# A graph network on one core: two pairs of VectorE steps change places in the attention stages

## The reference

```
# second layer: masked attention, 12 heads of 32
q, k, v = h @ Wq + bq, h @ Wk + bk, h @ Wv + bv
scores = q k^T / sqrt(32) + beta * adj ; where(adj > 0, scores, -9e15)
x = x + softmax(scores) v
# fourth layer: attention with an additive bias and an output projection
a = (h Wq^T)(h Wk^T)^T * 384**-0.5 + bias
a = where(all of a row == 0, -inf, a) ; a = nan_to_num(softmax(a))
x = x + (a v) Wo^T + bo
```

## Time and profile before

| | us |
|---|---|
| median of 3 runs | 2972.63 (2971.61 to 2974.18) |
| the profiled execution | 2975.63 |
| its span | 2973.9 |
| TensorE busy (matmul) | 2791.2 (94%) |
| VectorE busy | 1962.7 (66%) |
| ScalarE busy | 1033.1 (35%) |
| GpSimd busy | 950.6 (32%) |

### The profile page before, as it was taken

One profiled execution on the slowest core, in us unless ns is written; L12 is line 12 of the kernel. 1 busy time (PEld: TensorE's weight loads), 2 busy tenths in 40 slices (PEclk: granted clock), 3 DMA queues, 4 the chain that ended last, 5 costly groups with the idle time before them and its releaser, 6 DMA issues.

```text
span 2973.9 us, 64342 instructions
## 1 busy us (share of the span) xinstructions
PE 2791.2 (94%) x26048; PEld 2336.2 (79%) x26048; DVE 1962.7 (66%) x4550; ACT 1033.1 (35%) x1985; POOL 950.6 (32%) x874
## 2 busy tenths in 40 slices
PE   6999999999989999999999998999998799999997
PEld 5888878888868888887878877888887678777786
DVE  4444445555566777778676666676777777777775
ACT  2443333333334444443232322222222344343442
POOL 1222213444443333332010110343343444443443
PEclk9999999999999999999999999999999999999999
DMA  3222333333321121131211223223232011111011
GB/s 93 74 72 72 95 101 107 102 97 100 121 70 48 48 71 48 48 95 55 70 60 57 70 76 103 74 73 97 91 100 90 31 47 48 47 48 44 32 33 35
DMA packets 197320, 211.45 MB, mean 71 GB/s; under 512 B 72736, under 2 KB 197024, under 8 KB 197024
## 3 DMA queue, kind: packets, MB, share of 16 engines
q1 hardware_dynamic: 197024, 207.33, 22.7%
HBM read 131.80 MB, written 75.50 MB: 70 GB/s over the span
## 4 chain that ended last, share of the span: by engine, by line
PE 71%; DVE 17%; issue 8%; ACT 2%; POOL 2%; DMA 0%; DVEq 0%; SPq 0%; POOLq 0%; ACTq 0%
PE psum L672 27%; PE psum L675 26%; DVE v_x L1502 4%; PE psum L723 3%; PE psum L990 3%; DVE room L1650 2%; PE psum L660 2%; PE psum L840 2%; PE psum L885 2%; PE psum L829 2%; DVE room L1640 2%; DVE room L1533 2%; PE psum L739 1%; PE psum L861 1%; DVE fast L1373 1%
## 5 line engine op out<-in xcount | busy, mean ns | idle before, releaser
L675 PE MATMUL psum<-fast 128*128 128x384 f32 x5760 | 1128.4, 345 | 91.2 <-DVE room L1640 37.9
L675 PEld LDWEIGHTS psum<-fast 128*128 128x128 f32 x5760 | 994.6, 189 | 184.5 <-DVE room L1640 68.0
L672 PE MATMUL psum<-fast 128*128 128x512 f32 x3456 | 860.7, 400 | 11.6 <-ACT room L1191 4.9
L672 PEld LDWEIGHTS psum<-fast 128*128 128x128 f32 x3456 | 636.6, 189 | 166.6 <-issue 22.6
L1640 DVE TENSOR_TENSOR room<-psum,rows 128x384 f32<-128x384 f32 x384 | 212.6, 554 | 243.2 <-PE psum L675 134.7
L526 POOL TENSOR_TENSOR room<-room 128x768 f32<-128x768 f32 x128 | 188.6, 1474 | 419.3 <-DVE room L1539 260.7
L589 POOL TENSOR_TENSOR room<-room,halfs 128x4 f32<-128x4 f32 x32 | 32.4, 1012 | 688.0 <-DVE room L1673 688.0
L1135 ACT ACTIVATE room<-psum 128x512 f32<-128x512 f32 x192 | 114.5, 596 | 392.5 <-PE psum L672 392.5
L660 PE MATMUL psum<-mask,z_sb 128*128 128x128 f32 x1152 | 176.8, 284 | 50.7 <-ACT z_sb L1116 22.1
L1502 DVE TENSOR_TENSOR v_x<-psum,rows 64x192 f32<-64x192 f32 x512 | 181.4, 354 | 28.4 <-PE psum L675 23.2
L660 PEld LDWEIGHTS psum<-mask,z_sb 128*128 128x128 f32 x1152 | 129.6, 142 | 81.3 <-issue 27.6
(11 more groups left out here) (96 smaller groups left out, 3611.5 us busy)
## 6 DMA issues: line engine op xcount, KB each, us to landing
x_ring<-x_mid SPq DMA_DIRECT2D x64, 768.0 KB, 4.5
x_mid<-x_ring SPq DMA_DIRECT2D x48, 768.0 KB, 4.1
x_ring<-x_in SPq DMA_DIRECT2D x32, 768.0 KB, 4.6
z_mid<-x_ring SPq DMA_DIRECT2D x32, 768.0 KB, 4.2
z_sb<-z_mid SPq DMA_DIRECT2D x32, 768.0 KB, 6.4
out<-x_ring SPq DMA_DIRECT2D x16, 768.0 KB, 3.9
w_raw<-w_all SPq DMA_DIRECT2D x19, 576.0 KB, 7.2
adjc<-adj SPq DMA_DIRECT2D x64, 128.0 KB, 3.9
```

What stands on the lines that cost most here:

```text
L672: mm = nc.tensor.matmul(dst, wpart[s_][:, c, c_out * P:(c_out + 1) * P], hpart[:, c, 0:GT], start=(k == 0), stop=(k == 3 * C - 1))
L675: mm = nc.tensor.matmul(dst[:, 0:H], hpart[:, c, row:row + P], wpart[s_][:, c, :], start=(k == 0), stop=(k == 3 * C - 1))
```

## The change

Both edits are in VectorE's `a_body`, and both attention stages run it. The residual addition of tile 1, `a_add_x(g, 1)`, stands ahead of `a_sums(g, 3)` instead of behind it. The copy of the second value tile, `nat(1)`, stands ahead of the next group's first softmax tile, `a_soft(F, 0)`, instead of behind it. No instruction is added or taken away, and every other engine keeps its list. In the third stage `a_add_x` and `a_sums` issue nothing, so that only the second edit acts there.

```diff
                 next_w(F, X, 1)
                 low(0)
                 nat(0)
+                a_add_x(g, 1)
                 a_sums(g, 3)
-                a_add_x(g, 1)
                 low(1)
+                nat(1)
                 if F:
                     a_soft(F, 0)
-                nat(1)
                 a_keep_o(g, 2)
                 low(2)
                 if F:
                     a_sums(F, 0)
                 nat(2)
                 if F:
                     a_soft(F, 1)
                 a_add_x(g, 2)
                 a_keep_o(g, 3)
                 nat(3)
                 a_add_x(g, 3)
```

## The result

| | before | after |
|---|---|---|
| median, us | 2973.4 (2971.61 to 2974.18) | 3024.39 (3023.8 to 3026.01) |
| span of the profiled execution | 2973.9 | 3024.2 |
| mean granted clock | 0.992 | 0.986 |

The ratio is 1.0178 (95%: 1.0165 to 1.0192), slower by 51 us; 3027.3 was forecast. A period goes from one `a_out(g, 3)` to the next; undisturbed means that no stretch at half clock lies in it.

What follows compares the result with a forecast made beforehand. TensorE was taken to bound the kernel, VectorE's order counting where TensorE waits for it. Sixth-stage order +35.5, third stage -1 and clock +20.2 gave +54.7 on the median 2972.63: 3027.3 us, range 3003 to 3037, forecast chance 0.62.

Steps and rivals of the forecast that it cites:

- The order of the sixth stage: Sixth stage at full clock: later softmax tile delays `a_out(g, 3)` by 2.32 us a group; +35.5 us in all.
- The clock: Sixth stage: half-clock stretch behind the wait before `a_out(g, 3)` in 15 groups at 1.35 us each; +20.2 us.
- The third stage: Third stage: part 8 starts 0.70 us earlier, but part 9 waits for `low(2)`; -1 us, between -10 and +2.
- The addition: Sixth stage, `a_add_x(g, 1)` ahead of the sums: part 7 starts 0.61 us earlier, and the later sums cost nothing.
- The copy: Sixth stage, `nat(1)` ahead of `a_soft(F, 0)`: part 8 waits no more, but softmax tile and `a_out(g, 3)` come 2.32 us later.
- one idle time of 3.66: Sixth stage: part 9 ends about 2619.83, then TensorE stands 3.66 us in one piece before `a_out(g, 3)`.
- A: Sixth stage, rival: the clock holds at 2.4 GHz, so only the order costs; 3007.1 us, chance 0.2.
- B: Sixth stage, rival: slack before `a_out(g, 3)` absorbs the postponed softmax tile, 2.0 us won a group; 2941.6 us, chance 0.03.
- C: Sixth stage, rival: about half the delay absorbed by earlier exponents, 1.2 us a group, full clock; 2990 us, chance 0.06.
- D: Sixth stage, rival: two half-clock stretches a group, the second from the wait before `a_out(g, 2)`; 3050 us, chance 0.05.

Runs made afterwards that it cites:

- the run with the clock held: Changed kernel (both edits) plus unread matmuls on TensorE, five before part 9 and eight before `a_out(g, 3)`, in the sixth stage; ratio to before 1.0129, median 3013.4 us.
- the runs with the added matmuls: Unread matmuls in TensorE's waits before part 9 and `a_out(g, 3)`, added to the kernel with both edits (3013.4 us) and to that with the copy alone (3020.97 us).
- A new order: Kernel before with the sixth stage reordered on VectorE, GpSimd and ScalarE, including both swaps and `nat(2)` ahead of `a_sums(F, 0)`; ratio 0.9948, median 2958.15 us.
- The run with the next copy ahead of the sums: Changed kernel (both edits) with one more swap, `nat(2)` ahead of `a_sums(F, 0)` on VectorE; ratio to before 1.0065, median 2994.02 us.
- the new order on VectorE alone: Kernel before with only VectorE's part of the sixth-stage reordering, GpSimd and ScalarE as before; ratio 1.0160, median 3021.42 us.

## Why the prediction was right

The mechanism came out as it was written down, and the sum of +54.7 against +51.0 is closer than its terms. The order of the sixth stage was put at 35.5, with 0.5 for the last group; it is 35.0 without the last group, and 35.2 for the whole stage in the run with the clock held. The clock was put at 20.2 and is 13.7 in the loop and some 2 at the stage's two ends. The third stage was put at -1 and is +0.8, and the rest of the program, put at nothing, was 1.7 shorter in the profiled execution. That the last two nearly cancel is luck.

The addition. Expected: part 7 directly behind `a_score(F, 0)`, no cost in the sums. The rows show no wait before part 7, and the run with the addition alone that this gives nothing by itself. Right.

The copy. Expected: softmax tile 2.32 later, 5.46 and 6.14 unchanged, `a_out(g, 3)` 15.6 behind part 7. Measured: 5.46, 6.14, 15.60, undisturbed periods of 42.28 against 39.96, which is 2.32. Right to the hundredth: each term was a distance between two starts in one trace, or a duration from it, and none was guessed. (One figure is misread without effect: from the end of `nat(0)`, 2606.40, to 2607.89 it is 1.49; the 1.45 goes from the start of the sums.)

One wait was placed wrongly. The prediction had part 9 end at 2619.83 and one idle time of 3.66 before `a_out(g, 3)`. Part 9 of the sixth stage waits for `nat(2)`, which the sums hold up, and I didn't follow that semaphore. So the idle time is in two pieces, 1.50 and 2.03, with 1.9 us of work between them. It changes nothing in the order's cost, as both are ahead of the same start. But the term for the clock was argued from one wait of 3.66, which never occurs: the waits behind which the clock falls are of 2.03 to 2.06.

The clock. The term was mis-sized: 15 stretches at 1.35 were forecast, 20.2 us; it was nine in the loop at 1.52, 13.7. The price was too low and the count too high, two errors that work against each other: 15 at 1.52 would have been 22.8. The measured price lies between the 1.37 of the one row and the 1.7 of half speed over 3.4 us. That the stretches come of the waits is shown by the runs with the added matmuls. Why there are nine and not 15 stays open; that the idle time is in two pieces may be the reason, but no run tests it.

The third stage. Expected -1, within -10 and +2. The 14 groups gave 0.05 each, 0.7, and part 9 took over the wait as worked out. From the start of the stage to the first body of the next it is 0.8 longer, so the fifteenth group and the body behind it, which I had put at zero, cost about 1.5. Within the bounds, with the wrong sign.

The rivals. A (clock at full) would have been 3007; the run with the added matmuls is that case, 3013. The 6 us between them lie outside the sixth stage, which takes 35.2 more there against 35.5. B (the postponed tile absorbed) and C (half absorbed) are excluded by the unchanged 5.46 and 6.14. D (two stretches a group) did not happen.

## What to carry to other kernels

Before a step is moved ahead on an engine that works in order, ask what it waits for: everything behind it inherits that wait, and here a 1.5 us copy that waited for a projection held up the start of a chain over three engines. The waits of the bounding engine that such a move removes are worth nothing while a later wait of the same period ends a chain without slack; that last one has to be followed back first, and its start brought forward. A new order paid here only when the other queues followed it: the same VectorE order was 15 us faster than before with the two other queues moved and 48 us slower without.

## What the hardware showed

Waits of much the same length did very different things to the clock. In the groups with a stretch, the addition alone has a single wait, 2.19 before part 8, and a half-clock stretch begins behind it in 13 groups. The run with the next copy ahead of the sums stands longer in each group, 1.23 before `a_out(g, 2)` and 2.25 before `a_out(g, 3)`, and has two stretches in its loop. So the length of the wait doesn't decide it, nor the idle time of a group. What TensorE does ahead of the wait differs: turns and a mix of small matmuls in the first, nine full matmuls in the second. That this is the reason wasn't tested.

A stretch costs by where it falls: 1.52 of period in the changed kernel, where TensorE then waits for nobody until the next `a_out(g, 2)`; 0.66 with the addition alone in most groups, where the next wait takes up part of it; and nothing with the new order on VectorE alone, where the period that holds the row of 3.91 is 43.08 and the one ahead of it, without a stretch, 43.09.

The stretches can hold a period: with the copy alone, 13 periods in a row are 44.33 to 44.41 where the undisturbed one is 42.84, while both edits together change between 42.28 and 43.80. Why the one order is caught and the other not stays open.
